# The first attention's TensorE step: value and output projections ahead of the logits, and VectorE's add at the head of its step

## The reference, cut to what matters

```python
Q = jnp.einsum('bmd,hdk->bhmk', x, P_q)
K = jnp.einsum('bmd,hdk->bhmk', x, P_k)
V = jnp.einsum('bmd,hdv->bhmv', x, P_v)
logits = jnp.einsum('bhmk,bhnk->bhmn', Q, K) * math.sqrt(D_K)
logits = jnp.where(causal[None, None], logits, -jnp.inf)
key_weights = jax.nn.softmax(logits, axis=-1)
o = jnp.einsum('bhmm,bhmv->bhmv', key_weights, V)
y = jnp.einsum('bhmv,hdv->bmd', o, P_o)
...
x = _layernorm(x + y)
```

## Time and profile before

| | us |
|---|---|
| median of 3 runs (3773.41 to 3777.23) | 3773.79 |
| profiled execution, its own time | 3775.59 |
| its span, first to last instruction | 3773.8 |
| PE busy | 3586.4 (95%) |
| PEld busy | 3052.6 (81%) |
| ACT busy | 3373.2 (89%) |
| DVE busy | 3120.3 (83%) |
| POOL busy | 2748.7 (73%) |

### The profile page before, as it was taken

The page is one execution under the profiler, slowest core; times in us unless marked ns, Lnnn a source line. Parts: engine busy times, 40 slices in busy tenths (PEclk is TensorE's granted clock), DMA queues, the critical chain, the costliest instruction groups (busy, mean ns, idle before and its releaser), DMA issues.

```text
span 3773.8 us, 133054 instructions
## 1 busy us (share of the span) xinstructions
PE 3586.4 (95%) x47336; PEld 3052.6 (81%) x47336; DVE 3120.3 (83%) x6999; ACT 3373.2 (89%) x10923; POOL 2748.7 (73%) x2058
## 2 busy tenths in 40 slices
PE   7989979999999999999999999999999999999996
PEld 4666668888888888888888888888888888888885
DVE  7888978888888878888788887878888788888984
ACT  7888859989999999999999999899999999999994
POOL 0111159888788888888788888887888888888882
PEclk9999989999999999999999999999999999999998
DMA  2000001111111111111111111111111111111111
GB/s 98 7 11 12 7 23 46 34 33 32 40 46 34 35 31 34 43 41 40 29 36 36 40 46 33 32 31 40 46 35 36 29 35 41 34 34 38 40 37 33
DMA packets 165626, 132.97 MB, mean 35 GB/s; under 512 B 114928, under 2 KB 125552, under 8 KB 164720
## 3 DMA queue, kind: packets, MB, share of 16 engines
q1 hardware_dynamic: 164976, 124.45, 13.4%
HBM read 25.84 MB, written 4.19 MB: 8 GB/s over the span
## 4 chain that ended last, share of the span: by engine, by line
PE 71%; ACT 5%; issue 5%; DVE 5%; ACTq 0%; DVEq 0%; POOLq 0%; POOL 0%
PE bank L926 10%; PE bank L972 9%; PE bank L952 8%; PE bank L1011 8%; PE bank L994 6%; PE bank L891 4%; PE bank L892 4%; PE bank L893 4%; PE bank L865 4%; PE bank L987 3%; ACT a_E L1154 3%; PE bank L849 2%; PE bank L851 2%; PE bank L850 2%; PE bank L905 1%
## 5 line engine op out<-in xcount | busy, mean ns | idle before, releaser
L1208 POOL TENSOR_TENSOR a_rn<-a_ssqc,a_minus_half 128x16 f32<-128x16 f32 x384 | 1113.8, 2901 | 524.6 <-DVE a_ssqc L1379 519.2
L1154 ACT ACTIVATE a_E<-bank,a_negmax 128x96 f32<-128x96 f32 x3072 | 1015.5, 363 | 22.9 <-DVE a_negmax L1328 22.2
L1230 POOL TENSOR_TENSOR a_r<-a_u,a_rn 128x512 f32<-128x512 f32 x768 | 788.7, 1047 | 0.6
L1217 POOL TENSOR_TENSOR a_PN<-a_E,a_erec 128x384 f32<-128x384 f32 x768 | 743.2, 987 | 14.6 <-DVE a_erec L1387 14.5
L1154 ACT ACTIVATION_READ_ACCUMULATOR a_E<-bank,a_negmax 128x1 f32 x3072 | 705.7, 230 | 0.0
L1136 ACT ACTIVATE a_QK<-bank 128x512 f32<-128x512 f32 x768 | 467.1, 608 | 147.1 <-PE bank L926 147.1
L1341 DVE TENSOR_TENSOR a_u<-bank,a_rot_c 128x512 f32<-128x512 f32 x768 | 521.5, 679 | 2.4 <-ACT a_sq L1128 2.4
L1128 ACT ACTIVATE a_sq<-bank 128x512 f32<-128x512 f32 x768 | 483.5, 630 | 44.4 <-PE bank L893 13.7
L1351 DVE TENSOR_TENSOR a_v<-bank,a_rot_s 128x512 f32<-128x512 f32 x768 | 522.2, 680 | 0.0
L1112 ACT ACTIVATE a_PT<-bank 128x512 f32<-128x512 f32 x768 | 486.0, 633 | 25.1 <-PE bank L952 21.6
L926 PE MATMUL bank<-ident,a_r 128*128 128x128 f32 x3072 | 482.9, 280 | 18.1 <-DVE a_bias L1313 11.8
(11 more groups left out here) (140 smaller groups left out, 8412.7 us busy)
## 6 DMA issues: line engine op xcount, KB each, us to landing
a_V_even<-a_V_odd SPq DMA_DIRECT2D x384, 128.0 KB, 2.3
a_V_even<-a_V_odd SPq DMA_DIRECT2D x192, 64.0 KB, 2.1
a_raw<-in_qkv SPq DMA_DIRECT2D x20, 384.0 KB, 3.5
a_x_sh<-X SPq DMA_DIRECT2D x48, 128.0 KB
a_V_even<-a_V_odd SPq DMA_DIRECT2D x192, 32.0 KB, 2.0
a_f_sh<-X SPq DMA_DIRECT2D x48, 128.0 KB
a_x_sh<-X SPq DMA_DIRECT2D x48, 127.0 KB
a_f_sh<-X SPq DMA_DIRECT2D x48, 127.0 KB
```

Source lines behind the costliest of these rows:

```text
L1154: ins = act.activation(E[:, s.par, k, :], p_s[:, i % 2, col:col + KW], ACT.Exp, bias=negmax[:, s.par, k:k + 1], accum_out=esum[:, s.par, k ...
L1208: pool.tensor_tensor(rn[:, a.par, :], ssqc[:, a.par, :], minus_half[:, :], ALU.pow).then_inc(S["rn"], 1)
L1217: pool.tensor_tensor(PN[:, s.par, 2 * hp:2 * hp + 2, :].rearrange("p i (b k) -> p i b k", b=2)[:, :, :, 0:KW], spread(E[:, s.par, half, :] ...
L1230: pool.tensor_tensor(heads(r[:, a.par, half]), heads(u[:, a.par, half]), rn[:, a.par, mm * 2 * HG:(mm + 1) * 2 * HG].unsqueeze(2).to_broad ...
```

## The change

Two lists of calls are put in another order. No instruction is added or removed, and all semaphores and their counts stay.

```diff
@@ first_attention, TensorE's step
                     projected()
+                    values()
+                    transposes()
+                    out_projection()
                     logits(0)
                     logits(1)
-                    transposes()
-                    values()
-                    out_projection()
@@ first_attention, VectorE's step
+                    norms()
                     diagonals(0)
                     diagonals(1)
                     probs()
                     maxima(0)
-                    norms()
                     maxima(1)
```

## The result

| | before | changed |
|---|---|---|
| median | 3773.93 (3773.41 to 3777.23, 4 runs) | 3917.32 (3914.72 to 3919.95, 4 runs) |
| ratio, 95% interval | | 1.0378 (1.036 to 1.0396) |
| span of the profiled execution | 3773.8 | 3918.2 |

Slower by 143 us, 3.8%; 3913 was predicted. Where the time went is seen in three views.

A forecast was written before the change was run, and what follows sets the result against it. TensorE's own work was taken to bound the first attention, 3.20 us a step with transposes and 3.51 with values. Terms 71 + 3 + 15 + 50 = +139 us on 3773.79 gave 3913 us; 8-in-10 range 3850 to 3965.

The forecast's parts named there:

- The mechanism: First attention: TensorE's transposes and values wait for ScalarE's copies, now behind exponentials that need the later logits; forecast's chance 0.52.
- the rings: First attention: TensorE waiting for ScalarE's copies in transpose and value steps, plus delayed maxima: 71, 3 and 15 us.
- the clock: Steps with transposes: TensorE's clock falls after idle time, 0.9 us a step, +50 us in all.
- VectorE's move: Add, statistics and normalisation at the head of VectorE's steps 7, 8 and 10: costed at nothing.
- The transposes' ring: Transposes through both logits, maxima, exponentials and copy to the next transposes: 5.25 us even, 4.88 odd, against 3.20; +71 us.
- odd steps with values: Values wait for the previous V copy behind the first exponentials: 4.01 us against 3.51, 31 steps, +15 us.
- low_x: VectorE, step 8: waits for a later ScalarE copy and delays the next maxima some 0.5 us in six batches, +3 us.
- The steps behind the weights' split: Steps after the split of the next layers' weights: they lose their wait either way, so nothing was added.
- That the clock holds (3863): Rival: TensorE waits for the copies in first attention but its clock stays up, 3774 + 89 = 3863 us; chance 0.21.
- Low in nearly every step (3955): Rival: TensorE's clock is low in nearly every step with transposes, 3774 + 89 + 92 = 3955 us; chance 0.14.
- The faster rival: Rival: early transposes or values and output projection fill TensorE's waits of logits(0) for exponentials, 15 us, 3758 us; chance 0.05.
- The fourth rival: Rival: the values' wait hides and the transposes' loop is shorter than summed, no change to +60 us; chance 0.08.

The follow-up runs named there:

- filler run: Changed kernel plus 6 useless matmuls ahead of the projection in steps 6 to 13 of batches with transposes and step 3 of four batches: 3887.21 us.
- the run at 3762: Changed kernel with both ScalarE copies out of p_vt moved up, right behind its copy of the projection, ahead of both exponentials: 3761.95 us, ratio 0.9962.

## Why the prediction was right, term by term

The mechanism was right. The sum, 139 us against 143, is closer than its terms: the rings were put 24 us too low and the clock 19 too high, and that these nearly cancel is luck.

| term | predicted | measured |
|---|---|---|
| closed rings, all steps, full clock | 71 + 3 + 15 = 89 | 113 (filler run against before) |
| the clock | 50 | 31 (changed kernel against filler run) |
| VectorE's move | 0 | 0 (0.9988 to 1.0006) |

**The transposes' ring** was predicted at 5.25 and 4.88 us, and is 5.40 and 5.05. The pieces from VectorE's maxima to the copy were right. What was short is the output projection, taken at the 0.37 us that it has ahead of the next projection: ahead of the logits it takes 0.54 (428.51 to 429.05 above). A duration between two starts belongs to the pair, and the change made another pair. That is 0.15 to 0.17 us in each of 56 T steps, 9 us, and the same for odd steps with values, predicted at 4.01 and measured at 4.16.

**VectorE's diagonals** are the second piece that was short. `low_x` was taken at 0.5 us a batch, and the step that it delays, step 10, takes 6.24 us in the filler run, 1.2 over the 5.05 of its kind. These rows of that run show why (L399 is `low_x`, L432 the diagonals, L421 the maxima, L375 GpSimd's multiply):

```profile
412.90 0.69 DVE L399 TENSOR_TENSOR f_xl<-f_xt_sb,f_xh 128x512 fp32r<-128x512 f32 x1 [1.92 <-ACT f_xh L297]
413.30 1.20 POOL L375 TENSOR_TENSOR f_O<-f_V,f_prob_all 128x512 f32<-128x512 f32 x1 [3.39 <-PE bank L270]
413.50 0.70 PE L216 MATMUL bank<-f_QK 64*128 64x256 f32 x4
413.51 1.13 DVE L432 SCALAR_TENSOR_TENSOR f_diag_only<-f_E,ident 128x128 f32<-128x128 f32 x1
...
414.58 0.28 DVE L432 SCALAR_TENSOR_TENSOR f_diag_only<-f_E,ident 128x128 f32<-128x128 f32 x1
...
415.50 1.68 DVE L421 TENSOR_REDUCE f_negmax<-bank 128x1 f32<-128x256 f32 x4
```

The maxima start 2.00 us behind logits(0), and 0.80 in the odd step after (425.13 and 425.93). Of these 1.2 us, 0.85 is one instruction of the diagonals, 1.13 us long and not 0.28, while GpSimd's multiply runs beside it; about 0.35 is left for `low_x`, less than was predicted. The same makes step 6 take 5.70 us instead of 5.05 (6.06 in the fourth batch), which no term had: in the changed kernel the third instruction of the diagonals in step 5 takes 1.12 us (at 411.20, GpSimd's multiply from 411.09), and the maxima start 1.45 us behind logits(0). The prediction's ring enters VectorE only at its maxima; in these two steps VectorE comes to them late, and of GpSimd it asked only what its queue releases. Why the instruction is long beside the multiply no run tests. Over the batches step 6 comes to some 5 us and step 10 to some 4 more than predicted. With the 9 us of the output projection that is the shortfall of the T gates, 304 us in the filler run against 286; the other 6 are the V steps, the even ones at 3.60 us and not 3.51 among them.

**The steps behind the weights' split** were costed at nothing, on the ground that their wait was there before as well. At full clock that holds: in the fifth batch steps 2 and 3 together are 2.14 us over their kind before (9.15 and 7.01) and 2.31 in the filler run (10.08 and 7.77). What it left out is the clock. In the changed kernel the wait stands before the values in one piece of 2.14 us, before it was 1.23 and 0.65; the clock falls behind it, and the two steps take 11.65, in four batches 6 us more in all. By the first rows of steps 5 and 14 in the seven batches, 119 of the 144 us lie in the T steps (predicted 71 + 3 + 50 = 124) and 25 outside them (predicted 15).

**The clock** was mis-sized. I took 0.9 us a T step, a low stretch behind more than half of the gates. The price of one was right: 7.01 less 5.40 is 1.61, against 1.65. Their number was not: 17 of the 56 gates have one behind them. By the time between the first rows of steps 5 and 14, without fillers and with them (355 and 329 us in the seven batches), the clock costs 0.47 us a gate there. The sign given for it, a PEclk of the stage near 0.8, failed with it: 0.92. The even steps' idle time, 1.95 us above, is not enough by itself to bring the clock down each time; the same wait is followed by a low stretch in one step and not in another. The runs don't show what decides it. For the run with logits(0) ahead of the rings the gates idle 1.12 to 1.26 us (by its rows of L269 and L245), and its T steps at 4.69 and 4.82 us show no low stretch. But seven of its gates idle 1.52 us (step 10 of six batches, step 6 of the fourth), and three of these have one, so 1.95 us is no lower bound.

**The rivals.** That the clock holds (3863) falls short of both measured parts: the clock does fall, and with it held the time is 3887. The Trainium skill's rule (TensorE: Matmul & The Clock Gate, on drops in mid-kernel), by which gaps as short as these leave the clock alone, is not what the rows show: the fall to 0.50 stands behind an idle time of 1.95 us. Low in nearly every step (3955) is out by the count. The faster rival named a mechanism that is there: the logits' waits for exponentials shrank from 30.7 to 6.4 us. The gain shows only where the ring is open, which is the run at 3762. The fourth rival, a T ring shorter than its sum, is out: both kinds are longer than it.

## What to carry to other kernels

When work is moved ahead on one engine, look for the buffer that it writes and at which place of the other engine's list that buffer is freed. With one buffer, producer and consumer orders have to move together: here the same edit of TensorE is +143 us with the copies where they were, and -14 us with the copies ahead of the exponentials. To price such a ring, add its pieces once around, and take every piece between the neighbours that it will have.

## What the runs showed of the hardware

- Between matmuls over 128 rows and matmuls over 64 rows TensorE seems to lose time that shows in no wait: the output projection's four records take 0.37 us ahead of the projection and 0.54 ahead of the logits, and a step with four such changes took 3.83 us, with two 3.51. I have not measured it by itself.
- With 1.3 us of useless matmuls in each of 56 steps with a closed gate and in four more the kernel was 31 us faster: the clock stayed at 2.4 GHz there.
- The clock fell behind single idle times of 1.95 us, shorter than the 2.29 us seen before, but not each time; behind 1.52 us it fell in three steps of seven, in two of them with 1.30 us idle shortly ahead; it did not fall in the T steps behind 1.12 to 1.26 us.
- An instruction of VectorE's diagonals took 1.12 and 1.13 us where GpSimd's multiply ran at the same time; the others of the same steps took 0.28.
